# A 17x17 depthwise convolution on TensorE: output cells of 16 rows and four columns in place of 64 rows and two columns

## The chip, the core and the metric

One core of a Trainium2 chip runs the whole program. The metric is the time of one execution on the device, in microseconds (us), the median of several. A core has five engines that run beside each other and wait for one another through semaphores: TensorE (PE, a 128x128 array, with a queue of its own for loading weights, PEld), VectorE (DVE), ScalarE (ACT), GpSimd (POOL) and SyncE (SP, which here only issues transfers). Sixteen DMA engines move data between the device memory and the on-chip memory (SBUF, 128 partitions). TensorE writes to PSUM banks, which ACT and DVE empty.

## What is computed

Eight images of 96 channels and 64x64 pixels go through a convolution block and then through a bidirectional state-space mixer. The change lies in the first step of the first block; everything behind it stays.

```python
def _L0_conv_ref(x, plk_filter, ...):
    B, C, H, W = (8, 96, 64, 64)
    K = 17
    PAD = K // 2
    residual = x
    h = _bn(x, bn1_gamma, bn1_beta, bn1_mean, bn1_var)
    h = conv_general_dilated(h, plk_filter, window_strides=(1, 1),
            padding=[(PAD, PAD), (PAD, PAD)], feature_group_count=C)   # one 17x17 filter per channel
    h = einsum('bchw,dc->bdhw', h, pw_weight)
    h = _bn(h, bn2_gamma, bn2_beta, bn2_mean, bn2_var)
    h = gelu(h)
    ...                                  # squeeze and excite gives a factor a for each channel
    return residual + gamma * (h * a)
```

## The kernel before

The program is a chain of blocks with a barrier of all engines between them: `convolution`, `pointwise`, `normalise`, `scan` (by far the longest) and `output`. The convolution block is the first 513 us.

**Tiling.** A column pair (64 rows, two neighbouring columns) lies on the 128 partitions: partition = column parity x 64 + row. For one channel the 17x17 filter becomes nine matrices of 128x128 (`toep`, float32, banded), one for each horizontal shift of a column pair. The output of a channel, 128 partitions x 256 (8 images x 32 pairs), is the sum of nine products (L303), all into one PSUM bank `pc[c]`. A batch is four channels (CB = 4), so there are 24 batches.

**The matrices are made on the chip.** TensorE builds them (L282): `bands`, a 0/1 matrix for each output row y (102x128, bf16), picks filter taps out of `filt`, where the float32 taps stand as three bf16 parts on 3 x 34 partitions. A group is four rows y, 4 products of 72 columns into one bank `pw`; 16 groups make a batch's `toep`. ACT and DVE copy the groups out in turn (L200). The groups for batch s+1 stand between the products of batch s, one after every two shifts.

**The input.** `x_cols` is x laid out on the host as (parity, row), channel, image, pair. SP loads it by batches into two buffers `xraw` (L170 for batches 0 and 1, L176 for the others), one DMA of 128 rows x 4096 bytes for a batch. The load for batch s+2 is issued when the batch norm of batch s has read its buffer (`x_ready`). The loop also loads two batches past the end (batches 0 and 1 again), so 26 loads in all, and SP waits for the last of them (L178) before the block can end. DVE applies the batch norm (L259, 4 instructions for a batch) into `xpad`, whose outer columns are zero; it does so for batch s+1 once the products of batch s-1 are done, in the middle of its copies for batch s. The results go to `hs` (L205), which stays in SBUF for `pointwise`.

**Order on the queues.** Nothing is scheduled by a planner: every engine runs its own list in the order of the code, with hardware loops over pairs of batches. SP issues the constants first (three copies of the filter, each 34 rows of 6912 bytes, L164; `band` and masks; four vectors of batch norm, each copied to 128 partitions, L168), then batches 0 and 1 of x. DVE and ACT wait for all constants but one before their first work on them.

**pointwise.** TensorE turns `hs` round (L451, four transposes for a group of 512 columns), DVE copies, TensorE multiplies by the 96x96 weights (L445), ACT applies GELU (L519) into `act_out`; 64 groups. SP first issues some 70 small loads of constants for later (L428, L430), such as the state-space gather matrix and a_log (32 partitions each, read from DRAM as 8 blocks of 4 rows), then an image's result (L433).

## Times and profile before

| | us |
|---|---|
| median of 3 runs | 5830.08 (5827.94 to 5831.29) |
| the profiled execution: its time | 5833.66 |
| its span | 5831.9 |
| mean granted TensorE clock (share of 2.4 GHz) | 0.761 |

| stretch, us from the span's start | what runs |
|---|---|
| 0 to 41.4 | constants, preparation, first `toep` |
| 41.4 to 513.4 | 24 batches of the convolution |
| 513.7 to 639 | pointwise |
| 639 to the end | normalise, scan, output |

The profile is read so: a page with the busy time of each engine and with the span cut in 40 slices; groups of instructions by source line; tables of busy time in chosen stretches, with the granted TensorE clock, the mean busy share of the 16 DMA engines and the GB/s that they moved; and a timeline, instruction by instruction. "SPq" rows are DMA issues by SyncE, and the duration of such a row is that of the issue, not of the transfer. A "packet" is one piece that one DMA engine moves. Float32 products stand as two instructions each: 1728 rows of L303 are 864 products.

### The profile page before, as it was taken

What the parts mean: (1) busy time and instruction counts of PE and PEld (TensorE: products, weight loads), DVE (VectorE), ACT (ScalarE), POOL (GpSimd) and SP (SyncE); (2) the same over time, 40 slices, a digit from 0 to 9 for tenths busy, and PEclk for the clock granted to TensorE, in tenths of its full rate; (3) what the DMA queues carried; (4) which work ended last, traced back from release to release, by engine and by line L of the source; (5) the groups of instructions that cost most, each with busy time, mean ns of one, the idle gap of its engine ahead of it and who ended that gap; (6) DMA issues with size and microseconds to landing.
All of it is one profiled execution on the core that took longest, in us unless ns stands there. A gap on an engine that the chain in (4) does not pass through costs nothing. (4 is left out here: it accounts for less than half of the span.)

```text
span 5831.9 us, 75897 instructions
## 1 busy us (share of the span) xinstructions
PE 4650.0 (80%) x18020; PEld 1375.0 (24%) x18020; DVE 5255.8 (90%) x3583; ACT 3228.0 (55%) x5273; POOL 4947.2 (85%) x2349
## 2 busy tenths in 40 slices
PE   7998766777877888788788778787887878888877
PEld 5775311111111111111111111111111111111111
DVE  3322658999999999999999999999999999999998
ACT  1123755555565656655555655656556555556564
POOL 0000248999999999999999999999999999999998
PEclk9998886666677777777777777777777777777777
DMA  1011655555656666666666566665566666566666
GB/s 36 25 29 48 194 157 188 188 184 192 200 193 202 204 191 200 197 199 194 203 201 207 191 199 206 192 199 195 196 201 197 200 207 197 196 202 202 192 198 203
DMA packets 363220, 1050.78 MB, mean 180 GB/s; under 512 B 70868, under 2 KB 120294, under 8 KB 312604
## 3 DMA queue, kind: packets, MB, share of 16 engines
q1 hardware_dynamic: 354972, 1034.97, 55.5%
q10 hardware_dynamic: 8064, 14.16, 0.7%
q14 instruction: 166, 1.36, 0.1%
q8 instruction: 18, 0.29, 0.0%
HBM read 837.23 MB, written 211.63 MB: 180 GB/s over the span
## 5 line engine op out<-in xcount | busy, mean ns | idle before, releaser
L1405 POOL TENSOR_TENSOR hc<-hring,c_rep 128x1024 f32<-128x1024 f32 x1541 | 3599.7, 2360 | 74.7 <-DVE hring L1360 71.0
L1360 DVE TENSOR_TENSOR_SCAN hring<-decay,carry,u_ps 128x1024 f32<-128x1024 f32 x1221 | 2823.6, 2335 | 0.0
L1111 PE MATMUL u_ps<-stack_b,w_spread 48*128 48x512 bf16 x2442 | 995.4, 496 | 1005.3 <-DVE hring L1360 1001.4
L1342 DVE TENSOR_TENSOR u_ps<-u_ps,u_rep 128x1024 f32<-128x1024 f32 x1221 | 1478.0, 1211 | 72.6 <-DMA u_rep<-u_scr 55.6
L1236 ACT ACTIVATE decay<-dt_rep,w_a 128x1024 f32<-128x1024 f32 x1222 | 1396.4, 1145 | 224.4 <-DVE hring L1360 211.8
L1129 PE MATMUL y_ps<-hc,w_gather 128*32 128x512 f32 x6144 | 1131.9, 819 | 0.0
L1236 ACT ACTIVATE u_ps<-dt_rep,w_a 128x1024 f32<-128x1024 f32 x322 | 359.3, 1116 | 1102.6 <-DVE hring L1360 1102.2
L1392 POOL TENSOR_TENSOR drive_p<-u_rep,b_rep 128x1024 f32<-128x1024 f32 x322 | 760.4, 2362 | 10.1 <-DMA u_rep<-u_scr 10.1
L1360 DVE TENSOR_TENSOR_SCAN hring<-u_ps,carry,drive_p 128x1024 f32<-128x1024 f32 x321 | 752.0, 2343 | 0.0
L1111 PEld LDWEIGHTS u_ps<-stack_b,w_spread 48*128 48x128 bf16 x2442 | 144.9, 100 | 2369.6 <-DVE hring L1360 2168.7
L684 POOL TENSOR_TENSOR xs<-xc_ln,rs 96x512 f32<-96x512 f32 x64 | 89.9, 1405 | 707.1 <-ACT rs L668 693.4
L1152 PE MATMUL prep_ps<-xn,w_conv 128*128 128x512 f32 x792 | 477.3, 750 | 26.3 <-DMA xn<-xn_scr 24.7
L303 PE MATMUL pc<-xpad,toep 128*128 128x256 f32 x1728 | 469.3, 402 | 2.6 <-DVE toep L200 0.6
L200 DVE COPY toep<-pw 128x288 f32<-128x288 f32 x200 | 91.6, 458 | 327.5 <-PE pw L282 327.5
L1259 ACT ACTIVATE xc<-prep_ps,w_conv_b 128x512 f32<-128x512 f32 x198 | 135.7, 686 | 411.8 <-PE prep_ps L1152 395.9
L303 PEld LDWEIGHTS pc<-xpad,toep 128*128 128x128 f32 x1728 | 296.8, 191 | 37.6 <-issue 11.3
L1252 ACT COPY ends<-hring 128x1 f32<-128x1 f32 x1540 | 271.7, 176 | 0.0
L200 ACT COPY toep<-pw 128x288 f32<-128x288 f32 x200 | 79.6, 398 | 331.2 <-PE pw L282 331.2
L1129 PEld LDWEIGHTS y_ps<-hc,w_gather 128*32 128x32 f32 x6144 | 136.6, 123 | 500.2 <-issue 458.6
L1412 POOL TENSOR_TENSOR dt_sb<-soft,dt_sb 128x1024 f32<-128x1024 f32 (+1 forms) x130 | 235.9, 1815 | 4.0 <-ACT soft L1294 4.0
L1152 PEld LDWEIGHTS prep_ps<-xn,w_conv 128*128 128x128 f32 x792 | 172.3, 233 | 268.7 <-issue 238.4
L1416 POOL TENSOR_TENSOR soft<-dt_sb,xa 128x1024 f32<-128x1024 f32 (+1 forms) x130 | 235.2, 1810 | 0.2
(128 smaller groups left out, 4326.0 us busy)
## 6 DMA issues: line engine op xcount, KB each, us to landing
dt_rep<-dt_scr SPq DMA_DIRECT2D x194, 1024.0 KB, 5.8
u_rep<-u_scr SPq DMA_DIRECT2D x194, 1024.0 KB, 7.9
c_rep<-bc_scr SPq DMA_DIRECT2D x260, 512.0 KB, 4.9
b_rep<-bc_scr SPq DMA_DIRECT2D x130, 512.0 KB, 4.3
xn<-xn_scr SPq DMA_DIRECT2D x132, 384.0 KB, 5.2
y_scr<-y_sb SPq DMA_DIRECT2D x768, 64.0 KB, 2.0
xn<-xn_scr SPq DMA_DIRECT2D x132, 256.0 KB, 4.7
dt_scr<-dt_sb SPq DMA_DIRECT2D x260, 128.0 KB, 2.2
```

Source lines behind the costliest of these rows:

```text
L303: last = nc.tensor.matmul(pc[c][:, 0:B * XH].rearrange("p (b x) -> p b x", b=B), toep[par][:, n0:n0 + 2, :].rearrange("p a y -> p (a y)"), ...
L1111: mm = nc.tensor.matmul(u_ps[nv % NSLOT][:, sl], w["spread"][:, q, :], upper(stack_b[drv][:, sl]), start=True, stop=True)
L1129: last = nc.tensor.matmul(y_ps[at:at + 32, :], w["gather"][:, :], hc[n % NHC][:, i * SL:(i + 1) * SL], start=(q == 0), stop=(q == QN - 1))
L1152: mm = nc.tensor.matmul(prep_ps[:, :], w["conv"][:, j, 0:P], xn[:, j, PART[g]], start=(j == 0), stop=(j == 2))
L1236: nc.scalar.activation(to[:, :], dt_rep[r][:, b, :], ACT.Exp, scale=w["a"][:, col:col + 1]).then_inc(decay_ready, 1)
L1252: nc.scalar.copy(ends[:, drv, nv:nv + 1], hring[nv % NHR][:, end:end + 1]).then_inc(kept, 1)
L1342: nc.vector.tensor_tensor(slot[:, :], slot[:, :], u_rep[r][:, b, :], ALU.mult).then_inc(drive_ready, 1)
L1360: nc.vector.tensor_tensor_scan(hring[nv % NHR][:, ::step], factor[:, ::step], term[:, ::step], carry[:, drv, nv:nv + 1], ALU.mult, ALU.add ...
L1392: nc.gpsimd.tensor_tensor(drive_p[k % 2][:, :], u_rep[r][:, b, :], b_rep[q][:, :], ALU.mult).then_inc(pool_drive, 1)
L1405: nc.gpsimd.tensor_tensor(hc[nv % NHC][:, :], hring[nv % NHR][:, :], c_rep[q][:, :], ALU.mult).then_inc(c_applied, 1)
L1412: nc.gpsimd.tensor_tensor(dt_sb[:, HALVES[h]], soft[:, HALVES[h]], dt_sb[:, HALVES[h]], ALU.add).then_inc(dt_ready, 1)
L1416: nc.gpsimd.tensor_tensor(soft[:, HALVES[h]], dt_sb[:, HALVES[h]], xa[dr][:, HALVES[h]], ALU.mult).then_inc(u_ready, 1)
```

## The change

An output cell is now 16 rows by four columns (64 outputs) instead of 64 rows by two columns. What reaches it is a window of 32 rows (16 and 8 on either side) and, column-wise, five cells of four columns. So a channel takes five products instead of nine, but each makes only 64 of the 128 array columns; the image has four cell rows (NCY), and the even ones are written to PSUM partitions 0 to 63, the odd ones to 64 to 127 (`pc[c][64 * q:...]`), as two instructions that stand one behind the other. Each has 256 moving columns as before. The contraction side is 128: four columns x 32 rows.

- **Weights**: 16 rows y instead of 64, 2 column halves each: 32 products of 80 columns into 64 array columns for a batch (64 of 72 columns before), in four groups, one after the third cell of each channel. The taps come from `part`, which POOL copies out of `wide` (taps spread for the cells, zero elsewhere). ACT alone makes all copies out of PSUM, four of 320 columns and four of 256 for a batch.
- **Input**: `xraw` has for every cell row its own 32-row window, and every window twice (for the two halves of a cell's columns): 128 partitions x 4 cell rows x 4096 bytes, 1792 KB for a batch instead of 512 KB. A batch is loaded by 12 DMAs: 4 of 64 rows for the two inner cell rows, each reading DRAM as 2 (parities) x 32 rows, and 8 of 24 rows for the outer ones. The 26 loads, their order, the two buffers and the last wait stay.
- **Batch norm**: 24 instructions on 64 partitions for a batch (16 of 128 columns and 8 of 256, reading every second column), with a scale of zero where a window lies outside the image. DVE does nothing else in the loop.
- **Beginning**: POOL first zeroes the outer parts of `xraw`, for which SP waits ahead of the x loads; DVE zeroes `wide` and fills it, and makes 16 smaller `bands` rather than 64.
- **pointwise**: the columns of `hs` are picked in the new order, and the GELU writes runs of four neighbouring pixels instead of single ones 64 apart.

```diff
-NEAR = PAD // 2
-XP = XH + 2 * NEAR
+CY, CX = 16, 4
+ROWS = CY + 2 * PAD
+CELLS = 2 * PAD // CX + 1
+CELL = CELLS * CX
+NCY = H // CY
+NEAR = CELLS // 2
+XC = W // CX
+XP = XC + 2 * NEAR
...
+        X_DMAS = 2 * 2 + 2 * 4
...
+                rows = d["x_cols"].rearrange("(a y) c b x -> a y (c b x)", a=2)
+
+                def load(buf, at):
+
+                    for q in range(NCY):
+                        first = q * CY - PAD
+                        lo, hi = max(0, first), min(H, first + ROWS)
+                        if hi - lo == ROWS:
+                            for k in range(2):
+                                sp.dma_start(xraw[buf][2 * ROWS * k:2 * ROWS * (k + 1), q, :], rows[:, lo:hi, bass.ds(at, CB * B * XH)]).then_inc(x_in[buf], 16)
+                        else:
+                            for k in range(4):
+                                to = ROWS * k + lo - first
+                                sp.dma_start(xraw[buf][to:to + hi - lo, q, :], rows[k % 2, lo:hi, bass.ds(at, CB * B * XH)]).then_inc(x_in[buf], 16)
+
+                sp.wait_ge(raw_zero, 1)
                 for i in range(2):
-                    sp.dma_start(xraw[i][:, :, :, :], xk[:, i * CB:(i + 1) * CB, :, :]).then_inc(x_in[i], 16)
+                    load(i, i * CB * B * XH)
...
                         sp.wait_ge(x_ready, 2 * i + par + 1)
-                        sp.dma_start(xraw[par][:, :, :, :], xk[:, bass.ds(ch, CB), :, :]).then_inc(x_in[par], 16)
+                        load(par, ch * (B * XH))
                 for i in range(2):
-                    sp.wait_ge(x_in[i], 16 * (BATCHES // 2 + 1))
+                    sp.wait_ge(x_in[i], 16 * X_DMAS * (BATCHES // 2 + 1))
...
+                        for c in range(CB):
+                            evacuate_weights(s + 1, 1 - par, c, i + par)
+                            act.wait_ge(conv_done[par], CB * i + c + 1)
+                            nc.scalar.copy(hs[:, bass.ds((CB * s + c) * B * XH, B * XH)], pc[c][:, 0:B * XH]).then_inc(h_evac[c], 1)
...
-                    dve.wait_ge(x_in[buf], 16 * loads)
+                    dve.wait_ge(x_in[buf], 16 * X_DMAS * loads)
                     for c in range(CB):
                         at = s * CB + c
-                        last = nc.vector.tensor_scalar(xpad[buf][:, c, :, NEAR:NEAR + XH], xraw[buf][:, c, :, :],
-                                                       scale[:, bass.ds(at, 1)], shift[:, bass.ds(at, 1)], ALU.mult, ALU.add)
+                        for h in range(2):
+                            rows = slice(64 * h, 64 * h + 64)
+                            src = xraw[buf][rows, :, :].rearrange("p q (c b x) -> p q c b x", c=CB, b=B)
+                            for k, cells in enumerate((slice(0, 1), slice(1, NCY - 1), slice(NCY - 1, NCY))):
+                                last = nc.vector.tensor_scalar(xpad[buf][rows, c, cells, :, NEAR:NEAR + XC], src[:, cells, c, :, h::2],
+                                                               scale[rows, k, bass.ds(at, 1)], shift[rows, k, bass.ds(at, 1)], ALU.mult, ALU.add)
                     last.then_inc(x_ready, 1)
...
                     for r in range(YG):
-                        y = yg * YG + r
-                        last = nc.tensor.matmul(pw[bank][:, r * CB * FCOLS:(r + 1) * CB * FCOLS],
-                                                bands[:, y, :],
-                                                filt[:, bass.ds(s * (CB * FCOLS), CB * FCOLS)].bitcast(BF16)[:, 1::2],
-                                                start=True, stop=True, skip_group_check=True)
+                        for h in range(2):
+                            last = nc.tensor.matmul(pw[bank][64 * h:64 * h + 64, r * CB * CELL:(r + 1) * CB * CELL],
+                                                    bands[:, yg * YG + r, :, :].rearrange("p a y -> p (a y)"),
+                                                    part[buf][:, h, :],
+                                                    start=True, stop=True, skip_group_check=True)
...
-                            for k in range(SHIFTS):
-                                n0 = (c * SHIFTS + k) * 2
-                                last = nc.tensor.matmul(pc[c][:, 0:B * XH].rearrange("p (b x) -> p b x", b=B),
-                                                        toep[par][:, n0:n0 + 2, :].rearrange("p a y -> p (a y)"),
-                                                        xpad[par][:, c, :, k:k + XH],
-                                                        start=(k == 0), stop=(k == SHIFTS - 1))
-                                if k % 2 == 1:
-                                    weights(s + 1, after[c][k // 2])
+                            for k in range(CELLS):
+                                for q in range(2):
+                                    last = nc.tensor.matmul(pc[c][64 * q:64 * q + 64, 0:B * XH].rearrange("p (f b x) -> p f b x", f=2, b=B),
+                                                            toep[par][:, c * CELLS + k, :],
+                                                            xpad[par][:, c, q::2, :, k:k + XC],
+                                                            start=(k == 0), stop=(k == CELLS - 1))
+                                if k == 2:
+                                    weights(s + 1, 1 - par, c)
                             last.then_inc(conv_done[par], 1)
```

How the instructions stand. On SP, in the loop over pairs of batches (the ISA rows set registers), before:

```order
L176 ISA
L176 DMA xraw0<-in_x_cols 128x1024
L176 ISA
L176 DMA xraw1<-in_x_cols 128x1024
L171 REGISTER_ALU
```

and now, for the first batch of the pair:

```order
L199 ISA
L199 DMA xraw0<-in_x_cols 24x1024
L199 ISA
L199 DMA xraw0<-in_x_cols 24x1024 x3
L195 ISA
L195 DMA xraw0<-in_x_cols 64x1x1024 x2
L195 ISA
L195 DMA xraw0<-in_x_cols 64x1x1024 x2
L199 ISA
L199 DMA xraw0<-in_x_cols 24x1024
L199 ISA
L199 DMA xraw0<-in_x_cols 24x1024 x3
```

One issue for a batch has become twelve in a row, of two sizes; the shapes are those of the side in SBUF. On PE, within a batch, for a channel and a part of the next (the shapes are array columns x moving columns), before:

```order
L303 MATMUL pc<-xpad,toep 128x256 x2
L282 MATMUL pw<-filt,bands 128x72 x4
L303 MATMUL pc<-xpad,toep 128x256 x2
L279 REGISTER_ALU
L282 MATMUL pw<-filt,bands 128x72 x4
L303 MATMUL pc<-xpad,toep 128x256 x2
L282 MATMUL pw<-filt,bands 128x72 x4
L303 MATMUL pc<-xpad,toep 128x256 x3
```

and now:

```order
L361 MATMUL pc0<-xpad0,toep0 64x256 x6
L335 REGISTER_ALU
L340 MATMUL pw0<-part1,bands 64x80 x8
L361 MATMUL pc0<-xpad0,toep0 64x256 x4
L361 MATMUL pc1<-xpad0,toep0 64x256 x6
L340 MATMUL pw1<-part1,bands 64x80 x8
```

Sixteen small groups among 36 products have become four of eight among 40 (20 pairs) for a batch of four channels.

## Rows read from the trace of the kernel before

**Rows 1.** The page: span and slices (busy tenths, granted clock)
```profile
span 5831.9 us, 75897 instructions
...
PE   7998766777877888788788778787887878888877
...
PEclk9998886666677777777777777777777777777777
...
GB/s 36 25 29 48 194 157 188 188 184 192 200 193 202 204 191 200 197 199 194 203 201 207 191 199 206 192 199 195 196 201 197 200 207 197 196 202 202 192 198 203
```
**Rows 2.** Busy time by stretches: each engine, granted clock, DMA share, GB/s
```profile
core 0: us, PE busy (x) PEld busy (x) DVE busy (x) ACT busy (x) POOL busy (x), PEclk, DMA share, GB/s
...
100.00:200.00 100.00, 99.57 (x702) 79.19 (x701) 29.47 (x71) 20.05 (x51) 0.00 (x0) 1.00 0.09 26
200.00:300.00 100.00, 99.48 (x694) 78.85 (x694) 29.90 (x72) 20.05 (x51) 0.00 (x0) 1.00 0.09 26
```
**Rows 3.** Timeline of one channel within a batch: start, duration, engine, instruction
```profile
201.31 0.39 PEld L282 LDWEIGHTS pw<-filt,bands 102*128 102x128 bf16 x4
...
201.67 1.12 PE L303 MATMUL pc<-xpad,toep 128*128 128x256 f32 x4
...
202.41 0.39 PEld L282 LDWEIGHTS pw<-filt,bands 102*128 102x128 bf16 x4
...
204.95 1.54 PE L303 MATMUL pc<-xpad,toep 128*128 128x256 f32 x6
...
210.95 1.37 DVE L259 TENSOR_SCALAR xpad<-xraw,scale,shift 128x256 f32<-128x256 f32 x4
```
**Rows 4.** Groups by line, 0 to 513 us: busy, mean ns, idle before
```profile
L200 ACT COPY toep<-pw 128x288 f32<-128x288 f32 x200 | 79.6, 398 | 331.2 <-PE pw L282 331.2
...
L205 ACT COPY hs<-pc 128x256 f32 x48 | 17.9, 372 | 63.0 <-PE pc L303 63.0
...
L182 POOL COPY bands<-band 102x128 bf16<-102x128 bf16 x16 | 3.9, 289 | 18.5 <-DVE band L235 18.5
```
**Rows 5.** Timeline: the constants' issue and landing, first product, the block's end
```profile
0.75 0.20 POOL L188 MEMSET xpad<- 128x128 f32 x1 [0.29 <-POOLq L1638]
0.76 0.98 SPq L164 DMA_DIRECT2D filt<-in_filter_cols  x3
...
7.94 1.77 SPq L168 DMA_DIRECT2D bnp<-in_bn_mean  x1
9.75 2.04 SPq L168 DMA_DIRECT2D bnp<-in_bn_var  x1
11.82 2.03 SPq L170 DMA_DIRECT2D xraw<-in_x_cols  x2
...
19.49 0.29 DVE L235 CAST band<-band_f 102x254 bf16<-102x254 f32 x1 [18.52 <-DMA bnp<-in_bn_var]
...
32.63 1.52 DVE L259 TENSOR_SCALAR xpad<-xraw,scale,shift 128x256 f32<-128x256 f32 x4
...
41.43 2.05 PE L303 MATMUL pc<-xpad,toep 128*128 128x256 f32 x4 [0.60 <-DVE toep L200]
...
512.95 0.42 DVE L205 COPY hs<-pc 128x256 f32 x1 [0.17 <-PE pc L303]
513.67 0.34 SPq L428 DMA_DIRECT2D ident<-in_ident  x1
```
**Rows 6.** Busy time by stretches, as rows 2: tail of first loads; one later load
```profile
16.00:18.00 2.00, 0.00 (x0) 0.00 (x0) 0.00 (x0) 0.00 (x0) 0.00 (x0) 1.00 0.93 263
...
19.00:21.00 2.00, 0.00 (x0) 0.00 (x0) 1.48 (x7) 0.38 (x1) 1.15 (x5) 1.00 0.13 53
...
214.50:215.00 0.50, 0.50 (x7) 0.47 (x6) 0.26 (x1) 0.00 (x0) 0.00 (x0) 1.00 0.98 401
```
**Rows 7.** DMA view, 212 to 217 us: packets, and the one issue therein
```profile
DMA packets 144, 0.52 MB, mean 105 GB/s; under 512 B 16, under 2 KB 16, under 8 KB 144
...
xraw<-in_x_cols SPq DMA_DIRECT2D x1, 512.0 KB, 3.6
```
**Rows 8.** DMA view, 550.88 to 553.7 us: packets, and the four issues therein
```profile
DMA packets 160, 0.01 MB, mean 5 GB/s; under 512 B 160, under 2 KB 160, under 8 KB 160
...
a_log<-in_a_log SPq DMA_DIRECT2D x4, 3.0 KB
```
**Rows 9.** The scan: eight float32 instructions on 32 array columns each
```profile
3004.74 1.06 PE L1129 MATMUL y_ps<-hc,w_gather 128*32 128x512 f32 x8
```
**Rows 10.** pointwise, one group: product, transposes, GELU
```profile
586.09 1.02 PE L445 MATMUL pp<-ht,wpw 96*96 96x512 f32 x2
...
586.95 0.60 PE L451 MATMUL pt<-ident,hs 128*96 128x128 f32 x4
...
587.15 1.23 ACT L519 ACTIVATE act_out<-pp,bt 96x512 f32<-96x512 f32 x1
...
587.39 1.02 PE L445 MATMUL pp<-ht,wpw 96*96 96x512 f32 x2
```

More of the change, by code:

```diff
@@ L153, in convolution @@
         h_evac = [sem(f"h_evac{i}") for i in range(CB)]
-        xk = d["x_cols"]
         NCONST = 3 + 3 + 4
-        after = [range(NYG // CB * i, NYG // CB * (i + 1)) for i in range(CB)]
+        X_DMAS = 2 * 2 + 2 * 4
         with nc.Block() as block:
@@ L202, in evacuate_conv @@
[L202 to L221 removed]
+                    nc.gpsimd.memset(xraw[i][:, 0, :], 0.0)
@@ new lines, in _, with take @@
+                    last = nc.gpsimd.memset(xraw[i][:, NCY - 1, :], 0.0)
+                last.then_inc(raw_zero, 1)
+                for i in range(2):
+                    nc.gpsimd.memset(xpad[i][:, :, :, :, 0:NEAR], 0.0)
+                    last = nc.gpsimd.memset(xpad[i][:, :, :, :, NEAR + XC:XP], 0.0)
+                last.then_inc(pads_zero, 1)
+                pool.wait_ge(wide_ready, 5)
+                def take(s, buf):
+                    nc.gpsimd.tensor_copy(part[buf][:, :, :], upper3(wide[:, :, bass.ds(s * (CB * CELL), CB * CELL)])).then_inc(part_ready, 1)
@@ L223, in _ @@
+                take(0, 0)
+                take(1, 1)
+                with pool.Fori(0, BATCHES // 2) as i:
+                    for par in range(2):
+                        pool.wait_ge(w_ready, NYG * (2 * i + par + 1))
+                        take(2 * i + par + 2, par)
             @block.scalar
@@ L241, in _ @@
+                for y in range(CY):
+                    last = nc.vector.tensor_copy(bands[:, y, :, :], band[:, :, H - 1 - PAD - y:H - 1 - PAD - y + ROWS])
+                last.then_inc(band_ready, 1)
                 dve.wait_ge(filt_step, 1)
@@ L261, in batch_norm @@
                     last.then_inc(x_ready, 1)
[L263 to L266 removed]
                 batch_norm(0, 0, 1)
[L269 removed]
+                with dve.Fori(0, BATCHES // 2) as i:
+                    for par in range(2):
+                        wait(dve, conv_done[1 - par], CB * (i + par), True)
+                        batch_norm((2 * i + par + 1) % BATCHES, 1 - par, i + par + 1)
```

133 lines of the change are left out of this document (70 added, 63 removed).

## Prediction

> **What bounds the kernel now.** I read the slices of the page first: the convolution is in the first four, where PE is near full, the granted clock is 0.9 of 2.4 GHz and more in three, and the DMA moves 25 to 48 GB/s [rows 1]; what follows is bound by other engines and is not touched. Then the table of stretches: from 100 to 300 us PE is busy 99.5 of every 100 us at the full clock (1.00 is 2.4 GHz), DVE 30, ACT 20, and the DMA engines 9% at 26 GB/s [rows 2]. So the convolution is TensorE's own work, and everything else has room. The timeline says what that work is: six float32 instructions of 256 columns stand in 1.54 us and four in 1.12, so one more costs 0.21; from one weight group to the next are 1.10 us, and less four products (0.84) that leaves 0.26 for a group, 0.065 for each of its products [rows 3]. A batch is 72 x 0.21 + 64 x 0.065 = 19.3 us; 24 batches from 41.4 to 513.4 us are 19.7 each [rows 5].
>
> **TensorE after the change.** A batch has 40 products, 80 float32 instructions of 256 columns, and 32 weight products. If the halves of the array work side by side, that is 40 x 0.21 + 32 x 0.065 = 10.5 us, with the 0.4 a batch that the sum above falls short, 10.9. If they work one after the other it is 16.8 + 2.1 + 0.4 = 19.3. The scan has a case: eight float32 instructions of 512 columns on 32 array columns each stand in 1.06 us [rows 9], while two that use 96 columns take 0.86 from the first one's start to the transposes behind them, so eight would be 3.4 [rows 10]. They run side by side, so I take 10.9. The first guess would then be 24 x 8.8 = 211 us saved.
>
> **The other engines.** DVE: four batch norms of 256 columns take 1.37, about 0.32 each [rows 3]. A batch now has 8 of these and 16 of 128 columns, which cost between half and all of it: 5.1 to 7.7, I take 6. Every second element is read, which no row here shows; it would have to double the cost to matter. ACT: 4 x 0.40 x 320/288 + 4 x 0.37 = 3.3 us for a batch [rows 4]. POOL: one copy of 160 columns, under 0.4 by 0.29 for 128 [rows 4]. All are below 10.9. The start: POOL's four memsets of 1024 columns, at most eight times the 0.20 of 128 columns, end by 7 us, ahead of SP's first x load at 11.8; DVE's memset lies in its wait for the constants, which lasts until 19.5 [rows 5]. These cost nothing.
>
> **The loads.** Here the numbers stop being small. A batch brings 1792 KB instead of 512. Spread over all 16 engines that is nothing: in the thick of a load the chip shows 401 GB/s at a share of 0.98, 25.6 GB/s for each engine [rows 6], so 1.84 MB take 4.6 us, and twelve issues of 0.34 us (the last row of [rows 5]) 4.1 of SP. But are they spread? Three places say that it depends on the shape. First, the filter's three loads have 34 rows each, and they are the reason why constants take until 19.5 us [rows 5]. Behind them, from 19 to 21 us, only the tail of the first x loads runs: share 0.13 at 53 GB/s [rows 6]. 0.13 is two engines of 16, at 26.5 GB/s each: they are late by what 34 rows (2 x 17) left on them. Second, a load of 128 rows shows 144 packets, 16 of them under 512 bytes: 128 rows and, as I read it, one completion for each of 16 engines [rows 7]. Third, four loads of a_log, 32 rows in SBUF but read as 8 blocks of 4 rows, show 160 packets, 40 each: 32 rows and 8 completions [rows 8]. 16 divides 32, yet only 8 engines worked: the outer dimension of the side in DRAM, 8, set it.
>
> The inner loads of the change have 64 rows in SBUF and 2 blocks of 32 rows in DRAM. By the same pattern they run on **two engines**. Each puts 32 rows x 4096 bytes on each of the two, four of them 524,288 bytes. The outer ones (24 rows) run on 12 engines, 2 rows each, if the largest divisor up to 16 counts: 8 x 8192 = 65,536 more. Together 589,824 bytes on each of two engines for a batch: at 26.5 GB/s 22.3 us, at 25.6 23.0. The 53 is a rounded number and each engine has twelve completions besides; I take **22.4 us a batch**.
>
> The Trainium skill states this as a rule, in "DMA: Bandwidth & Descriptors", section "Why a DMA increments its semaphore by 16 and not by 1": a copy runs on the largest number up to 16 that divides the slowest dimension of both sides. By that rule the inner loads get 2 engines and the outer ones 12; the trace agrees in its 8 engines for [8, 4] against 32 and its two for 34 rows. That page's ceiling, 435 GB/s for 16 engines or 27.2 for each, would make the batch an estimated 21.7 us.
>
> 22.4 is more than any engine needs, and it hides the rest. TensorE waits half its time; even at 1.2 GHz throughout, 2 x 10.5 + 0.4 = 21.4 would fit, and so would halves one after the other at the full clock. Is the pair of engines ever idle? Load s+2 is issued when the batch norm of s ends, 6 us after load s landed and 16 us before load s+1 is through, and SP needs 4 to 5 us to issue it: a cover of 11 us. SP may be held: four loads of batch norm's vectors took some 2 us each to issue, against 0.34 for the last row [rows 5]; but what holds it is a full queue, which keeps the engines fed.
>
> **The sum.** The x loads stand behind the constants on the same two engines, whose last landed at 19.5 us; from there 26 loads, since SP waits for the two extra ones as well. 19.5 + 26 x 22.4 = 601.9 us. Batch 23's data lands at 557.1, its norm, products and copies end by 576, inside that. The block's end then takes the 0.3 us that lie between DVE's last copy and SP's next issue now (513.4 to 513.7) [rows 5]: 602.2 against 513.7, **+88.5 us**.
>
> pointwise: the product and four transposes fill PE's period of 1.30 us, and the GELU's 1.23 and its gap fit it exactly [rows 10]. How long a GELU takes that writes runs of four is in no row; faster, it gains nothing while PE has no slack, and slower it costs 64 times its excess over 1.3. It touches no more places than now, so I take 0, between -5 and 5. The transposes read with the same stride. Block by block the rest is as before, since the barrier passes the shift on whole. The span of 5831.9 becomes 5920.4. The profiled execution took 5833.7, 3.6 above the median of 5830.1; moved by the same, the median is **5918.6 us**.
>
> **Rivals.** *The loads are spread after all* (the address generation joins dimensions, or the block count doesn't rule where the SBUF side is 64). For it: nothing in these rows; only small loads show the 8. Then TensorE sets the pace: start about 38.6 (DVE's chain ends at 32.6 as before [rows 5], then 6 of norm), 24 x 10.9 = 261.6, end 300.5, -213: **5617 us**. The point from which it decides: to be no later than now, 26 T must stay below 494, T = 19.0 us or 503,000 bytes on the busiest engine at 26.5. Two engines have 590,000; four would have 328,000, 12.4 us, the end at 342 and 5658.
>
> *Spread, and the halves don't overlap*: 24 x 19.3 from 38.6 ends at 502, -12 (5818); with less of a gain in the weights it is within 0.2%. [rows 9] speak against it.
>
> *Two engines, and slower than their tail showed.* In the busiest 2 us the 16 engines gave 263 GB/s at 0.93, 17.7 each, with many small packets among them [rows 6]. At that rate 33.3 us a batch, 885 in all: 6201. The x rows are 4096 bytes, as in the 25.6 case, so I hold it for a far bound. A nearer form is a gap of 1 us a batch where two loads meet: +26, 5945.
>
> **How the numbers follow.** Two engines at 22.0 to 23.5 us a batch: 0.79, 5905 to 5950. Two engines and slower than that: 0.06. Spread, TensorE the bound (5617 to 5660): 0.12. Spread, no overlap: 0.03, half of it within 0.2%. About 0.2% (12 us) is what a measurement of this kernel can tell from no change. So slower 0.85, same 0.02, faster 0.13. The range reaches from the cases' lower edge, with 5 us for pointwise, to that with gaps: 5898 to 5965. It holds some 0.82.
>
> **What would show it.** In the profile after: the share of the DMA engines at about 0.20 and 82 GB/s through the block (1.84 MB by 22.4 us) in place of 0.09 and 26; TensorE busy about half of it; DVE's norm (L316) waiting for xraw, about 22.4 us from batch to batch; a window with one inner load that counts 64 + 2 packets; SP's last wait until about 602 us. If the period is 10.9 us and DVE waits for PE, the first rival holds. If TensorE's instructions stand at 0.21 each and not in pairs, the overlap is wrong, and it won't show in the time. What would make all of it wrong is an engine pair that runs above 31 GB/s, or loads joined by address.

## The result, and the profile after

| | us | ratio to before |
|---|---|---|
| before, median of 4 runs | 5830.68 (5827.94 to 5834.40) | |
| after, median of 4 runs | 5958.11 (5956.34 to 5959.55) | 1.0218 [1.0205, 1.0231] |
| the profiled execution after: its time, its span | 5957.61, 5955.8 | |

The change makes the kernel 2.2% slower, by 127 us; the forecast was 88.5. Direction and mechanism came out as forecast, the size was nearly one and a half times as large. The page of the kernel after the change shows where (slices as in [rows 1]; the groups are those of batch norm and of the convolution's products, with the idle time ahead of them and what ended it):

```profile
span 5955.8 us, 75684 instructions
...
PE   3455575777788787787778878877878778878877
...
PEclk8777787666677777777777777777777777777777
...
GB/s 74 79 76 76 93 215 157 185 185 186 192 203 202 194 194 201 198 197 197 197 200 199 198 200 199 200 204 203 196 196 197 199 202 204 196 194 200 198 198 200
...
L316 DVE TENSOR_SCALAR xpad<-xraw,scale,shift 64x128 f32<-64x128 f32 (+1 forms) x600 | 186.8, 369 | 414.2 <-DMA xraw<-in_x_cols 411.5
L361 PE MATMUL pc<-xpad,toep 128*64 128x256 f32 x1920 | 283.0, 445 | 304.4 <-DVE xpad L316 304.4
```

TensorE, full in the first slices of before, is now three to five tenths busy. It waits 304 us for the batch norm, and the batch norm waits 411 us for `xraw`. The stretches (as [rows 2]) show what the loads do:

```profile
100.00:200.00 100.00, 50.53 (x472) 33.99 (x474) 29.96 (x97) 13.14 (x33) 1.29 (x4) 0.70 0.23 79
...
317.50:321.50 4.00, 4.00 (x34) 2.66 (x33) 0.00 (x0) 0.80 (x2) 0.00 (x0) 0.71 0.57 169
321.50:341.50 20.00, 6.95 (x82) 4.86 (x80) 7.48 (x24) 2.40 (x6) 0.32 (x1) 0.71 0.13 53
```

A batch has two phases. For 20 us, the inner loads, the share is 0.13 at 53 GB/s: two engines of 16, as in the tail that stood in [rows 6]. For some 4 us, the outer loads, it is 0.57 at 169. The mean is 0.23 at 79 GB/s. The DMA view of 322.0 to 327.2 us, in the inner phase, counts 64 packets of 4096 bytes, as many as one such load has, and three completions:

```profile
DMA packets 67, 0.26 MB, mean 50 GB/s; under 512 B 3, under 2 KB 3, under 8 KB 67
```

The timeline of one batch, and the block's end:

```profile
298.13 2.41 PE L361 MATMUL pc<-xpad,toep 128*64 128x256 f32 x20
...
300.50 2.41 PE L361 MATMUL pc<-xpad,toep 128*64 128x256 f32 x20
...
308.97 7.58 DVE L316 TENSOR_SCALAR xpad<-xraw,scale,shift 64x128 f32<-64x128 f32 x24 [16.46 <-DMA xraw<-in_x_cols]
...
316.80 2.83 PE L361 MATMUL pc<-xpad,toep 128*64 128x256 f32 x12 [12.84 <-DVE xpad L316]
...
320.84 15.21 SPq L195 DMA_DIRECT2D xraw<-in_x_cols  x4
...
333.15 7.59 DVE L316 TENSOR_SCALAR xpad<-xraw,scale,shift 64x128 f32<-64x128 f32 x24 [16.60 <-DMA xraw<-in_x_cols]
...
645.97 0.38 SPq L486 DMA_DIRECT2D ident<-in_ident  x1
```

Batch norms start 24.1 us apart. Twenty float32 instructions, the ten products of a channel in both halves, stand in 2.41 us: ten pairs, side by side. The first channel after the wait runs slower (12 instructions in 2.83 us, where 20 take 2.41). TensorE had been idle for 12.8 us before, and the granted clock is 0.50 (1.2 GHz) from 309 to 319 us and 1.00 (2.4 GHz) from 320 to 325; the 0.71 in the rows above is the mean of both levels. It costs nothing here, since the next load is late anyway. SyncE spends 15.21 us on issuing the four inner loads of a batch: it is held up. The first experiment, e1_spread, shows that it can go faster: there eight loads of 32 rows and one of 24 take it 4.17 us. Pointwise begins at 645.97 us where it began at 513.67 [rows 5], +132.3. What follows takes 5309.8 us instead of 5318.2, 8.4 less; 132.3 less 8.4 is the 123.9 by which the spans differ.

### The profile page after: what moved, and what is told of

It reads as the page before. It is cut to its first block and busy times, and to the rows that moved or that the text cites. A ratio compares the mean times of both kernels' runs of the same rounds, so it can differ in the third digit from the quotient of the medians.

```text
span 5955.8 us, 75684 instructions
## 1 busy us (share of the span) xinstructions
PE 4445.9 (75%) x17412; PEld 1182.8 (20%) x17412; DVE 5295.9 (89%) x3820; ACT 3187.4 (54%) x5221; POOL 4961.5 (83%) x2363
## 5 line engine op out<-in xcount | busy, mean ns | idle before, releaser
L316 DVE TENSOR_SCALAR xpad<-xraw,scale,shift 64x128 f32<-64x128 f32 (+1 forms) x600 | 186.8, 369 | 414.2 <-DMA xraw<-in_x_cols 411.5
L361 PE MATMUL pc<-xpad,toep 128*64 128x256 f32 x1920 | 283.0, 445 | 304.4 <-DVE xpad L316 304.4
L1212 PE MATMUL prep_ps<-xn,w_conv 128*128 128x512 f32 x792 | 476.4, 748 | 25.2 <-DMA xn<-xn_scr 23.5
L250 ACT COPY toep<-pw 128x320 f32<-128x320 f32 x100 | 42.4, 426 | 450.9 <-PE pw L340 450.9
L361 PEld LDWEIGHTS pc<-xpad,toep 128*64 128x64 f32 x1920 | 162.1, 160 | 377.9 <-issue 341.8
```

Of the source, the lines that this page charges most:

```text
L361: last = nc.tensor.matmul(pc[c][64 * q:64 * q + 64, 0:B * XH].rearrange("p (f b x) -> p f b x", f=2, b=B), toep[par][:, c * CELLS + k, :], ...
L1212: mm = nc.tensor.matmul(prep_ps[:, :], w["conv"][:, j, 0:P], xn[:, j, PART[g]], start=(j == 0), stop=(j == 2))
```

## The experiments

Theory: an inner load, read from DRAM as 2 blocks, runs on two engines, and these set the period. Rivals: the bytes themselves, or the size on the SBUF side. Two things beside it were in dispute: why the period is 24.1 us and not 22.4, and whether the pairing of halves is worth anything. Blocks of code are cut to what differs; "period" is the distance of two batch norms. Where a ratio is given, four or five executions were timed, otherwise one; executions of one kernel lie some 0.2% apart.

### One load for each window half (e1_spread)

```diff
-                        if hi - lo == ROWS:
-                            for k in range(2):
-                                sp.dma_start(xraw[buf][2 * ROWS * k:2 * ROWS * (k + 1), q, :], rows[:, lo:hi, bass.ds(at, CB * B * XH)]).then_inc(x_in[buf], 16)
-                        else:
-                            for k in range(4):
-                                ...
+                        for k in range(4):
+                            to = ROWS * k + lo - first
+                            sp.dma_start(xraw[buf][to:to + hi - lo, q, :], rows[k % 2, lo:hi, bass.ds(at, CB * B * XH)]).then_inc(x_in[buf], 16)
```

> The four inner loads of a batch (64 rows in SBUF, read from DRAM as 2 blocks of 32 rows) are cut into eight of 32 rows, each with one block of 32 rows as its source. The bytes, the windows loaded twice and everything else stay; a batch is loaded by 16 DMAs instead of 12. Theory (the two blocks of the source put an inner load on two engines): 32 rows over 16 engines leave 2 rows on each, and the outer loads 2 on each of 12, so the busiest engines carry 16 + 16 rows, 2*8 + 2*8 = 32 packets of 4096 bytes a batch, 5.1 us at 0.159 us each. TensorE then sets the pace: 40 pairs of 0.21 us, 32 weight products and some 0.4 are 9.9 to 10.9 us a batch in place of 24.1, the convolution block ends at 277 to 300 us instead of 646, DVE waits for PE and not for xraw, and the run takes 5590 to 5620 us. Rival (the bytes, 1792 KB a batch, or the SBUF side hold the loads back, however they are cut): the period stays at 22 to 24 us and the run at 5940 to 5960. Rival (SP's issues hold them back): 16 issues of about 0.45 us are 7.2 us a batch, below the 9.9, so they would show only if one costs 0.7 or more: 11 to 13 us a batch, 5650 to 5690.

Measured: 5584.49 us, ratio to before 0.9583 [0.9567, 0.9599]. The stretch from 100 to 200 us, two batch norms, and the start of pointwise:

```profile
100.00:200.00 100.00, 100.00 (x1189) 70.38 (x1186) 79.50 (x256) 33.48 (x84) 3.21 (x10) 1.00 0.78 194
...
163.62 7.58 DVE L312 TENSOR_SCALAR xpad<-xraw,scale,shift 64x128 f32<-64x128 f32 x24 [1.92 <-PE pc L357]
173.05 7.58 DVE L312 TENSOR_SCALAR xpad<-xraw,scale,shift 64x128 f32<-64x128 f32 x24 [1.85 <-PE pc L357]
...
268.19 0.37 SPq L482 DMA_DIRECT2D ident<-in_ident  x1
```

The period is 9.46 us (from 163.62 to 220.42 six batches), a little under the 9.9 to 10.9 that were expected, and so is the time. TensorE is busy throughout at the full clock, DVE waits for PE, and the block ends 378 us earlier than in the changed kernel. The same bytes, cut by four more instructions a batch, are no limit. What I had not expected is the DMA share: 0.78, where 194 GB/s at the rate of [rows 6] would be 0.47.

### The number of blocks in DRAM (e_g4, e_g2)

From e1_spread, with nothing changed on the SBUF side (e_g2: g=2 and 0:16):

```diff
+                            src = rows[k % 2, lo:hi, bass.ds(at, CB * B * XH)]
+                            if hi - lo == ROWS:
+                                src = rows[k % 2, :, bass.ds(at, CB * B * XH)].rearrange("(g y) n -> g y n", g=4)[:, 0:8, :]
```

> The kernel of e1_spread, but each of the eight inner loads of 32 rows reads DRAM as 4 blocks of 8 rows that lie 16 rows apart, so that two cell rows get other input rows than they should: that part of the convolution is computed on wrong rows. Number, size and place in SBUF of the loads are those of e1_spread. Theory (the number of blocks in DRAM sets the number of engines): four engines, 8 rows on each; 8 x 8 + 8 x 2 = 80 packets of 4096 bytes a batch on the busiest, 12.7 us at 0.159 us, and up to 14.3 with what the small loads cost more in between: period 12.7 to 14.3, the convolution block ends at 350 to 395, DMA share about 0.4 in it, the run 5670 to 5705 us. Rival (only the 64 rows on the SBUF side, or the rows loaded twice by one instruction, were the cause): as e1_spread, 9.9 to 10.9 us a batch and 5590 to 5620.

> The kernel of e1_spread, but each of the eight inner loads of 32 rows reads DRAM as 2 blocks of 16 rows that lie 32 rows apart, so that two cell rows get other input rows than they should: that part of the convolution is computed on wrong rows. Theory (blocks in DRAM set the engines): two engines, 8 x 16 + 8 x 2 = 144 packets of 4096 bytes a batch on each, as in the changed kernel: 22.4 to 24.5 us a batch, block end 600 to 655, 53 GB/s at a share of 0.13 while inner loads run, the run 5920 to 5970 us. Rival (the size of the SBUF side): as e1_spread, 5590 to 5620.

Measured: 5738.71 and 5969.40 us. From 100 to 200 us in e_g4, 3 us of its inner phase and a pair of batch norms, then stretch and batch norms of e_g2:

```profile
100.00:200.00 100.00, 72.19 (x700) 48.91 (x698) 50.22 (x161) 19.97 (x50) 2.56 (x7) 0.84 0.39 118
...
306.00:309.00 3.00, 0.06 (x2) 0.00 (x0) 2.95 (x11) 0.37 (x1) 0.00 (x0) 0.99 0.26 104
...
175.47 7.67 DVE L315 TENSOR_SCALAR xpad<-xraw,scale,shift 64x128 f32<-64x128 f32 x24 [8.01 <-DMA xraw<-in_x_cols]
191.12 7.58 DVE L315 TENSOR_SCALAR xpad<-xraw,scale,shift 64x128 f32<-64x128 f32 x24 [7.98 <-DMA xraw<-in_x_cols]
```

```profile
100.00:200.00 100.00, 47.19 (x451) 31.06 (x452) 30.93 (x100) 12.78 (x32) 1.28 (x4) 0.70 0.22 74
...
191.74 7.57 DVE L315 TENSOR_SCALAR xpad<-xraw,scale,shift 64x128 f32<-64x128 f32 x24 [17.10 <-DMA xraw<-in_x_cols]
216.00 7.57 DVE L315 TENSOR_SCALAR xpad<-xraw,scale,shift 64x128 f32<-64x128 f32 x24 [16.69 <-DMA xraw<-in_x_cols]
```

Same number of loads, bytes and places in SBUF: with one block the period is 9.5 us (and PE's), with four blocks 15.7, with two 24.3 to 24.7. The block count rules, and the rivals are out. e_g2 came within what was expected; e_g4 did not (5670 to 5705 us were, with 12.7 to 14.3 us a batch). Its 80 packets are 12.7 us at 0.159, and the outer loads cost 1.3 more than that counts (next section); the other 1.7 us of its period stay unexplained. The Trainium skill's rule, in "DMA: Bandwidth & Descriptors", section "Why a DMA increments its semaphore by 16 and not by 1", on which the prediction leaned beside the rows, gives 16, 4 and 2 engines for these three. The traces agree: in the inner phase e_g4 shows a share of 0.26 (four engines of 16) at 104 GB/s and e_g2, from 205 to 215 us, 0.14 at 54; the 0.78 of e1_spread takes more than twelve.

### What an outer load costs (e_inner, e_act, e_mix, e_o2)

e_inner drops the eight outer loads. In e_act ACT issues them:

```diff
-                    for q in range(NCY):
+                    for q in range(1, NCY - 1):
...
+                            if c == 0:
+                                act.wait_ge(x_ready, 2 * i + par + 1)
+                                load_outer(par, (2 * i + par + 2) % BATCHES * CB * (B * XH))
```

In e_mix SyncE issues one inner and two outer loads in turn; in e_o2 the outer loads too have 2 blocks (of 12 rows):

```diff
+                    for n, q in enumerate((1, 1, 2, 2)):
+                        ...
+                        outer(0, n)
+                        outer(NCY - 1, n)
```

```diff
+                                src = rows[k % 2, :, bass.ds(at, CB * B * XH)].rearrange("(g y) n -> g y n", g=2)[:, 0:12, :]
```

> The changed kernel without the eight outer loads of a batch; the outer cell rows of the input stay zero, so that part of the convolution is left out. It measures what the outer loads cost in the period of 24.1 us. The four inner loads are 128 packets of 4096 bytes on each of two engines. Expected if an outer load costs only its two packets on each engine (my forecast, 2.5 us for the eight): 21.5 us a batch, block end at 580, the run 5890 us. Expected if the outer phase really costs the 4 us that the trace of the changed kernel shows: 20.0 to 20.4 us a batch, block end at 540 to 550, the run 5850 to 5865 us.

> The changed kernel, with the eight outer loads of a batch issued by ScalarE (after its first copy of weights of the batch) instead of SyncE; the inner loads stay on SyncE in the same form. It asks where the 1.7 us a batch come from by which the period (24.1 us) exceeds my forecast (22.4). Theory 1 (SyncE needs 0.45 us or more for each of eight outer loads and does so when the two engines have run empty, so their phase lasts 4.1 us where the engines need 2.5): with two issuers the two engines always have work, the period falls to 22.4 to 22.9 us, the block end from 646 to 602 to 615, the run from 5958 to 5915 to 5928 us. Theory 2 (packets take longer when twelve engines move data at once, whoever issues): the period stays at 23.8 to 24.3 and the run within 8 us of 5958.

> The changed kernel with the same twelve loads for a batch in another order on SyncE: one inner load and two outer ones, four times, in place of four outer, four inner, four outer. Theory 1 (the two busy engines run dry while SyncE issues eight outer loads one behind the other, 0.45 us each): an inner load of 5.1 us now covers the issues of two outer ones, so the period falls from 24.1 to 22.4 to 22.9 us a batch and the run from 5958 to 5915 to 5930 us. Theory 2 (while twelve engines move the rows of an outer load, each packet takes 0.22 to 0.25 us in place of 0.16, whoever issues them and when): the period stays at 23.8 to 25.2 and the run at 5950 to 5990 us. The run with ScalarE as second issuer (25.2 us a batch) speaks for the second.

> The changed kernel, but each of the eight outer loads of 24 rows reads DRAM as 2 blocks of 12 rows that lie 32 rows apart: the outer cell rows are computed on wrong rows. It asks why an outer load costs the two busy engines 0.47 us (24.07 us a batch with them, 20.33 without) where its two packets are 0.32. Two engines now carry 12 rows each for such a load, 8 x 12 + 128 = 224 packets of 4096 bytes a batch, 35.5 us at 0.1585. Theory 1 (every load costs an engine some 0.15 us besides its packets): 35.5 + 12 x 0.01 to 0.15 = 36.2 to 37.3 us a batch. Theory 2 (packets are slower only while twelve engines work at once): with two engines at work throughout, 35.4 to 35.8 us a batch; block end at 940 to 950 and the run 6252 to 6262 us, against 6270 to 6300 by the first.

Measured: e_inner 5861.90 us; e_act 5990.70, ratio 1.0271 [1.0254, 1.0288]; e_mix 5952.61; e_o2 6257.96. Two batch norms of each, in that order:

```profile
162.08 7.58 DVE L312 TENSOR_SCALAR xpad<-xraw,scale,shift 64x128 f32<-64x128 f32 x24 [12.78 <-DMA xraw<-in_x_cols]
182.38 7.58 DVE L312 TENSOR_SCALAR xpad<-xraw,scale,shift 64x128 f32<-64x128 f32 x24 [12.72 <-DMA xraw<-in_x_cols]
```

```profile
177.13 7.57 DVE L332 TENSOR_SCALAR xpad<-xraw,scale,shift 64x128 f32<-64x128 f32 x24 [17.62 <-DMA xraw<-in_x_cols]
202.50 7.58 DVE L332 TENSOR_SCALAR xpad<-xraw,scale,shift 64x128 f32<-64x128 f32 x24 [17.81 <-DMA xraw<-in_x_cols]
```

```profile
165.45 7.58 DVE L318 TENSOR_SCALAR xpad<-xraw,scale,shift 64x128 f32<-64x128 f32 x24 [16.18 <-DMA xraw<-in_x_cols]
189.35 7.58 DVE L318 TENSOR_SCALAR xpad<-xraw,scale,shift 64x128 f32<-64x128 f32 x24 [16.32 <-DMA xraw<-in_x_cols]
```

```profile
268.93 7.58 DVE L317 TENSOR_SCALAR xpad<-xraw,scale,shift 64x128 f32<-64x128 f32 x24 [28.06 <-DMA xraw<-in_x_cols]
304.50 7.58 DVE L317 TENSOR_SCALAR xpad<-xraw,scale,shift 64x128 f32<-64x128 f32 x24 [27.99 <-DMA xraw<-in_x_cols]
```

Periods of 20.3, 25.4, 23.9 and 35.6 us. So the eight outer loads cost 24.1 - 20.3 = 3.8 us, 0.47 each, where their two packets on each engine should be 0.32. It is not SyncE: with its issues behind the inner loads (e_mix) nothing is gained to speak of, and with a second issuer it gets worse (neither of the periods expected for e_act came, nor their times). My first explanation, formed on the trace of after, that the two engines run empty while SyncE issues, falls. Nor is it a fixed cost for each load: in e_o2, where only two engines ever work, 224 packets take 35.6 us, 0.159 each, with nothing left over for twelve loads. What is left is that a packet takes longer while the loads on twelve engines run. The number of engines alone does not do it: with all sixteen at work in [rows 6] a packet took 0.16 us (0.98 x 16 engines x 0.5 us, over the 49 packets that 401 GB/s are). Why e_act is 1.3 us a batch above the changed kernel I did not settle.

### What makes packets slow in the small loads (e1_step, e1_far)

From e1_spread; e1_step, then e1_far:

```diff
-                            to = ROWS * k + lo - first
-                            sp.dma_start(xraw[buf][to:to + hi - lo, q, :], ...
+                            to = lo - first
+                            sp.dma_start(xraw[buf][k::4, q, :][to:to + hi - lo, :], ...
```

```diff
-rows[k % 2, lo:hi, bass.ds(at, CB * B * XH)]
+rows[k % 2, lo:hi, bass.ds(at if k < 2 else far, CB * B * XH)]
```

> The kernel of e1_spread, but each load of 32 (or 24) rows goes to every fourth partition instead of 32 neighbouring ones, so that the rows lie in other places than the products want: the convolution is computed on rows out of place. Bytes, packets, number of loads and source stay. In e1_spread a packet of 4096 bytes took about 0.28 us while loads ran (0.16 in the single load of 128 rows of the kernel before), and the DMA engines were busy 0.78 of the time at 194 GB/s. Theory (sixteen engines that write into the same 32 partitions hold one another up): spread over all partitions the packets take 0.16 to 0.18 us again, the share falls to about 0.5 at the same 194 GB/s. Rival (it is the many small loads, two packets for each engine): 0.25 to 0.29 us and 0.78 as before. TensorE sets the pace in either, so the time stays within 8 us of 5584.

> The kernel of e1_spread, but the windows that a batch loads a second time (loads 2 and 3 of each cell row) come from a batch twelve further on, so that no two loads of a batch read the same addresses; the odd column halves of each cell are computed on wrong data. It asks why a packet took 0.22 to 0.29 us in loads of 24 or 32 rows on 12 or 16 engines, and 0.16 in a single load of 128 rows. Theory (loads in flight at once read the same 4096-byte rows twice, and hold one another up): packets 0.16 to 0.18 us, the DMA share between 100 and 200 us at 0.50 instead of 0.78, at the same 194 GB/s. Rival (many loads of two packets for an engine, whatever they read): 0.25 to 0.29 us and 0.75 to 0.80. The time stays within 8 us of 5584 in either, since TensorE sets the pace.

Measured: 5661.00 and 5580.88 us. The DMA view gives the packets and their share of 16 engines' time; of the changed kernel from 317.5 to 321.5 us, of e1_spread from 100 to 200, of e1_step from 100 to 300 and of e1_far from 100 to 200:

```profile
DMA packets 231, 0.68 MB, mean 169 GB/s; under 512 B 66, under 2 KB 66, under 8 KB 231
...
q1 hardware_dynamic: 231, 0.68, 56.6%
```

```profile
DMA packets 7121, 19.42 MB, mean 194 GB/s; under 512 B 2381, under 2 KB 2381, under 8 KB 7121
...
q1 hardware_dynamic: 7121, 19.42, 77.6%
```

```profile
DMA packets 10361, 28.30 MB, mean 141 GB/s; under 512 B 3456, under 2 KB 3456, under 8 KB 10361
...
q1 hardware_dynamic: 10361, 28.30, 48.3%
```

```profile
DMA packets 7064, 19.29 MB, mean 193 GB/s; under 512 B 2356, under 2 KB 2356, under 8 KB 7064
...
q1 hardware_dynamic: 7064, 19.29, 75.0%
```

Share x 16 x time over the packets that are no completions: 36.2 us by 165 is 0.22 us in the changed kernel's outer phase, 0.26 in e1_spread (not the 0.28 of the expectation), 0.22 in e1_step, 0.25 in e1_far. Next to these stands the 0.16 of [rows 6], but that is the best half microsecond of a load. The same sum over the whole of that load of 128 rows, in the window of [rows 7], gives 0.23:

```profile
q1 hardware_dynamic: 144, 0.52, 37.0%
```

(0.370 x 16 x 5 us over 128 packets; from 212 to 214 us the share is 0.35 at only 41 GB/s, from 214.5 on it is 0.98 at 401.) So a load of 128 rows has its slow packets too, at its beginning, and a load that leaves two packets on each engine may be all beginning. Engines that start from rest hardly explain e1_spread, though, where they are busy 0.78 of the time and a packet takes 0.26. Reading the same rows twice is at most a small part of it (e1_far). e1_step is inconclusive: packets are shorter but not 0.16, and the run brought an effect that I had not foreseen. Its period is 12.5 to 13.3 us, set by the issues, and its time lies 69 us above the 5592 that either theory allowed: SyncE took 4.42 us for five loads of 24 rows in

```profile
152.29 4.42 SPq L195 DMA_DIRECT2D xraw<-in_x_cols  x5
...
152.49 1.61 SPq L195 DMA_DIRECT2D xraw<-in_x_cols  x4
```

(the first row is e1_step's, the second e1_spread's): 0.9 us for a load of 24 rows to every fourth partition, against 0.4 to neighbours. So its engines also had less to do at once, which alone may shorten packets. The cause stays open. The Trainium skill, in "SBUF — State Buffer", section "Door 1: The DMA port swizzle (why [64,N] ≈ [32,N])", says that partitions 0 to 31 and 32 to 63 reach the same 8 of 16 ports. By it 16 engines that write 32 neighbouring partitions share ports in pairs, and a packet would take up to twice 0.16, an estimate; the 0.22 to 0.26 would fit. No run here separates it from other effects of many small loads, and no row says which partitions an engine writes at a time, so e1_step may have left the sharing as it was.

### The order of the halves (e_serial)

From e1_spread, where TensorE sets the pace:

```diff
-                            for k in range(CELLS):
-                                for q in range(2):
+                            for q in range(2):
+                                for k in range(CELLS):
...
-                                if k == 2:
+                                if q == 0:
                                     weights(s + 1, 1 - par, c)
```

> The kernel of e1_spread with the ten products of a channel in another order: the five of the even cell rows (array columns 0 to 63), then the five of the odd ones (64 to 127), so that neighbouring products use the same half of the array. The input is fast here, so TensorE's time is seen in the run. Theory (two products on different halves run at the same time, one after the other on one half): 80 instructions of 0.21 us and the weights are 17 to 19 us a batch instead of 9.5, the convolution block about 180 to 230 us longer, the run 5770 to 5815 us. Rival (the halves have nothing to do with it, a product on 64 array columns is simply half as long): as e1_spread, 5584 within 10 us.

Measured: 5715.07 us, ratio to before 0.9803 [0.9787, 0.9820], 131 us above e1_spread. Two batch norms, five instructions of one half, and a longer stretch with both:

```profile
173.11 7.58 DVE L312 TENSOR_SCALAR xpad<-xraw,scale,shift 64x128 f32<-64x128 f32 x24 [7.12 <-PE pc L357]
187.74 7.59 DVE L312 TENSOR_SCALAR xpad<-xraw,scale,shift 64x128 f32<-64x128 f32 x24 [7.05 <-PE pc L357]
```

```profile
199.96 1.27 PE L357 MATMUL pc<-xpad,toep 128*64 128x256 f32 x5
...
203.63 3.09 PE L357 MATMUL pc<-xpad,toep 128*64 128x256 f32 x17
```

The period is 14.7 us against 9.46, and a single instruction on one half still takes its 0.22 us (five start within 0.9 and end after 1.27). So the gain is from running two at once, and the rival falls. But the period is shorter than the 17 to 19 us that I expected, and the time 55 us under the range: where the order passes from one half to the other, the first instructions of the new half run beside the last of the old one. 17 instructions stand in 3.09 us, where one after the other they would take 3.7.

### The first microseconds (e1_filt) and the last load (e_nolast)

From e1_spread:

```diff
-                    sp.dma_start(filt[i * FROWS:(i + 1) * FROWS, :], d["filter_cols"]).then_inc(const_in, 16)
+                    sp.dma_start(filt[i * FROWS:i * FROWS + 32, :], d["filter_cols"][0:32, :]).then_inc(const_in, 16)
+                    sp.dma_start(filt[i * FROWS + 32:(i + 1) * FROWS, :], d["filter_cols"][32:FROWS, :]).then_inc(const_in, 16)
```

e_nolast (from the changed kernel; the same in DVE's loop, whose last norm then stands behind it):

```diff
-                with sp.Fori(0, BATCHES // 2) as i:
+                with sp.Fori(0, BATCHES // 2 - 1) as i:
...
-                    sp.wait_ge(x_in[i], 16 * X_DMAS * (BATCHES // 2 + 1))
+                    sp.wait_ge(x_in[i], 16 * X_DMAS * (BATCHES // 2))
```

> The kernel of e1_spread, and the three filter loads of 34 rows x 6912 bytes each cut into one of 32 rows and one of 2. My reading of the first microseconds was that 34 rows run on two engines (17 rows of 6912 bytes on each, three times: 353 KB, 13.8 us at 25.6 GB/s) and are the reason why the constants are complete only at 19.0 us. Expected by it: 32 rows lie on 16 engines (2 rows each), the filter is there some 2 us after its issue, and DVE's first step on it moves from 19.0 to 13 to 15 us, where the last batch norm vector (issued until 11.6) sets it; everything behind starts 4 to 6 us earlier, and the run takes 5576 to 5581 us against 5584.5 of e1_spread. Rival (the four vectors, each copied to 128 partitions in 128 packets of 384 bytes, are what takes until 19 us): DVE starts within 1 us of 19.0 and the run stays at 5584.

> The changed kernel without the two loads past the last batch, and without the batch norm that reads them. By my sum the block lasts 26 loads since SyncE waits for the extra two. Expected: the last load is complete two periods of 24.1 us earlier (597), but batch 23's norm, products and copies follow, 7.6 + 10.9 + 1 = 19.5 us, so the block ends at 616 to 618 instead of 645.97 and the run takes 5928 to 5931 us, 29 less. Rival (products or copies set the end anyway): no change, 5958.

Measured: e1_filt 5571.80 us, ratio to before 0.9560 [0.9547, 0.9573], the fastest of all; e_nolast 5927.62. From e1_filt's timeline, and the start of pointwise in e_nolast:

```profile
4.94 0.43 SPq L186 DMA_DIRECT2D bnp<-in_bn_var  x1
...
11.87 2.02 DVE L272 SCALAR_TENSOR_TENSOR hs<-filt,masks 102x1728 f32<-102x1728 bf16 x1 [6.03 <-DMA bnp<-in_bn_var]
```

```profile
615.66 0.38 SPq L488 DMA_DIRECT2D ident<-in_ident  x1
```

With 32 rows on 16 engines the filter no longer holds the queue: the last batch norm vector is issued in 0.43 us at 4.94 instead of in 2.04 at 9.75 [rows 5], and DVE starts at 11.87 where it started at 19.0 in e1_spread. That fits the reading that 34 rows run on two engines, and that a full queue is what made those issues long. The gain is larger than expected (DVE at 13 to 15 us, 4 to 6 us in all): the block ends 8.0 us earlier; the other 4.6 us of the 12.7 between the medians lie behind it, and I have no reason for them. e_nolast ends its block at 615.7, 0.3 us below the 616 to 618 that were expected: SyncE's wait for two loads that nobody uses is worth 30 us.

## Why the prediction was right, and where its size was off

**Two engines.** Right, and shown: 0.13 at 53 GB/s for 20 us of each 24 in the trace, and the period follows the number of blocks in DRAM (e1_spread, e_g4, e_g2). That the change is slower though its TensorE work halved hangs on this step alone.

**22.4 us a batch.** This is the term that was mis-sized: it measured 24.08. Its two parts were 19.9 us for the inner loads and 2.5 for the outer ones. e_inner measures 20.3 for the first: 128 packets at 0.159, the rate of 25.6 GB/s; I had leaned to the 26.5 of a rounded 53. The second is 3.8, since an outer load costs 0.47 us and not 0.32. I had priced its packets at the rate of the two engines' tail and of the best half microsecond of one wide load, and these are slower. [rows 2] had the sign of it: a share of 0.09 at 26 GB/s is 0.23 us a packet, over whole loads. The period is 1.7 us above 22.4, times 26 loads 44 us, which is all of the difference at the block's end: 88.5 + 44 = 132. The main case, 22.0 to 23.5 us a batch and 5905 to 5950 us, was therefore missed. The 5958 us lie in the range of 5898 to 5965 only through the room that was left above it for gaps, and there were no gaps: that part is luck.

**Cover.** The prediction gave the queue 11 us and said that the engines stay fed. From 305 to 345 us, in slices of 1 us, the DMA engines of the changed kernel never move less than 49 GB/s, and e_mix, which hides the issues otherwise, moves the period by 0.2 us, so this held. The rival of "a gap of 1 us a batch" named the right size (5945) for a wrong reason: there is no gap.

**26 loads from 19.5 us.** 19.5 + 26 x 24.08 = 645.6, and pointwise starts at 645.97. That the two extra loads count is shown by e_nolast. (DVE and ACT in fact wait for all nine constants; "all but one" in the part on the kernel is a slip, and the count in the code, 10 less one, is those nine.)

**TensorE.** Side by side: right. 10.9 us a batch was too much; it is 9.46 where nothing else limits (e1_spread). A pair takes 0.22, as forecast, but the weight products pair up too and take 0.14 us for eight, not 0.52 (from one channel to the next are 300.50 - 298.13 = 2.37 us, and ten pairs are 2.23 of it), and the 0.4 that I added is not there.

**DVE, ACT, POOL.** DVE's batch norm takes 7.58 us, the upper end of 5.1 to 7.7 rather than 6. ACT's copies are as forecast (426 ns). None of it shows in the time, as the prediction said.

**pointwise.** 0 was taken, between -5 and 5; it takes 122.2 us instead of 125.5. The GELU's 64 instructions with runs of four:

```profile
L579 ACT ACTIVATE act_out<-pp,bt 96x512 f32<-96x512 f32 x64 | 49.9, 779 | 46.7 <-PE pp L503 27.9 <-DMA act_scr<-act_out 18.8
```

They are 779 ns long where they were 1.23 us [rows 10], and ACT now waits for PE, whose 1.30 us a group are the bound as before; so the gain stays small. The other 5 us by which the rest got shorter I can't name. In e_mix, with the same code behind the block, the rest took 5306.7 us, in e1_spread 5312.0: it moves by some us from one program to the next.

**The rival that the loads are spread.** It gave 5617 us at a chance of 0.12. Made true by e1_spread it is 5584; the mechanism was right, and the rest is TensorE's 1.4 us a batch.

## What to carry to other kernels

Before counting a DMA's bytes, read how many engines will carry it. Here the outermost dimension in DRAM decided (2 or 4 blocks, against 32 rows), and one instruction that takes a short outer dimension along ("2 halves x 32 rows") can cost more than two instructions with the long dimension alone. Here that one choice turns a gain of 246 us into a loss of 127. A DMA share of 0.13 that lasts is the mark of it, and the place to look first when engines wait for a load far under the peak rate. And a price taken from the best half microsecond of a wide load is too low for small ones, and for the whole of the wide one too.

## What the runs showed of the hardware that I had not expected

- Packets of 4096 bytes took 0.16 us wherever only two engines worked and in the thick of a load of 128 rows, but 0.23 on average over the whole of that load and 0.22 to 0.26 in loads of 24 and 32 neighbouring rows on 12 or 16 engines; e1_spread needs a DMA share of 0.78 for 194 GB/s. The cause is open.
- SyncE takes 0.4 us to issue a load of 24 rows to neighbouring partitions and 0.9 us to every fourth one, and that alone set e1_step's period.
- Products on different halves of the array overlap without being strictly alternate: five products of one half and then five of the other still gave 14.7 us a batch, where 80 instructions of 0.22 one after the other would be 17.6.
- ScalarE's GELU over 512 columns takes 0.78 us where it writes runs of four elements and 1.23 where each element goes to a place of its own.
